# Fused self attention, cross attention and feed forward on one core: the first stage's q, k and v weights loaded and split by column quarters

## The reference

```python
h = _ln(x, g1, be1)
x = _attn(h, h, Wq1, Wk1, Wv1, Wo1, bo1) + x          # self attention
h = _ln(x, g2, be2)
x = _attn(h, context, Wq2, Wk2, Wv2, Wo2, bo2) + x    # cross attention
h = _ln(x, g3, be3)
y = h @ Wp + bp
a, gate = (y[..., :FF_HID], y[..., FF_HID:])
x = a * jax.nn.gelu(gate, approximate=False) @ W2 + b2 + x
# _attn: q = x@Wq, k = ctx@Wk, v = ctx@Wv; softmax(q k^T * DHEAD**-0.5) v; out @ Wo + bo
```

## Time and profile before

| | |
|---|---|
| median of 3 runs | 3026.1 us (3021.39 to 3029.89) |
| profiled execution | 3024.38 us, span 3022.6 us |
| PE busy | 2958.4 us (98% of the span) |
| DVE, ACT, POOL busy | 76%, 62%, 47% |
| first matmul on real data | 16.27 us after the span's start |

### The profile page before, as it was taken

The page is one execution under the profiler, slowest core; times in us unless marked ns, Lnnn a source line. Parts: engine busy times, 40 slices in busy tenths (PEclk is TensorE's granted clock), DMA queues, the critical chain, the costliest instruction groups (busy, mean ns, idle before and its releaser), DMA issues. The chain is left out here.

```text
span 3022.6 us, 77287 instructions
## 1 busy us (share of the span) xinstructions
PE 2958.4 (98%) x25480; PEld 2579.0 (85%) x25480; DVE 2304.4 (76%) x3858; ACT 1878.4 (62%) x5618; POOL 1429.0 (47%) x976
## 2 busy tenths in 40 slices
PE   7999999999999999999999999999999979999999
PEld 6888888888888888788888888888888858888888
DVE  5877777777777777788888888888888856666664
ACT  6666666666666666677777777777777733232322
POOL 4555555555555555555555555555555531111110
PEclk9999999999999999999999999999999989999999
DMA  7787878788887887888888888888888841112211
GB/s 239 228 243 243 243 244 244 243 243 246 244 245 240 245 247 239 261 252 256 253 253 254 253 254 253 254 251 260 251 252 254 248 148 56 56 62 62 69 56 35
DMA packets 475243, 640.79 MB, mean 212 GB/s; under 512 B 58944, under 2 KB 405952, under 8 KB 474944
## 3 DMA queue, kind: packets, MB, share of 16 engines
q1 hardware_dynamic: 473824, 639.96, 69.8%
q10 hardware_dynamic: 1376, 0.27, 0.1%
HBM read 338.57 MB, written 301.47 MB: 212 GB/s over the span
## 5 line engine op out<-in xcount | busy, mean ns | idle before, releaser
L602 POOL TENSOR_TENSOR at_probs<-at_probs,at_row_inv 128x1024 f32<-128x1024 f32 x512 | 969.6, 1894 | 1059.5 <-DVE at_row_inv L808 1059.4
L653 ACT ACTIVATE at_probs<-at_ps_s,at_neg_max 128x256 f32<-128x256 f32 x2048 | 945.7, 473 | 143.2 <-DVE at_neg_max L781 94.7
L781 DVE TENSOR_REDUCE at_neg_max<-at_ps_s 128x2 f32<-128x512 f32 x1024 | 660.4, 684 | 194.7 <-PE at_ps_s L959 191.1
L800 DVE STREAM_TRANSPOSE at_blocks<-at_probs 128x1024 f32<-128x1024 f32 x512 | 630.8, 1232 | 2.1 <-POOL at_probs L602 2.0
L706 ACT ACTIVATE at_qk_hi<-at_ps_qk 128x512 fp32r<-128x512 f32 x512 | 305.7, 597 | 324.5 <-PE at_ps_s L959 183.4
L978 PE MATMUL at_ps_o<-at_probs_t,at_v 128*64 128x256 f32 x4096 | 500.9, 386 | 1.9 <-DMA at_probs_t<-at_turns 1.9
L891 PE MATMUL at_ps_qk<-at_h_hi,w_hi 128*128 128x256 f32 x1536 | 432.1, 304 | 12.7 <-ACT at_h_hi L676 6.2
L653 ACT ACTIVATION_READ_ACCUMULATOR at_probs<-at_ps_s,at_neg_max 128x1 f32 x2048 | 414.6, 202 | 0.0
L978 PEld LDWEIGHTS at_ps_o<-at_probs_t,at_v 128*64 128x64 f32 x4096 | 271.9, 137 | 148.6 <-issue 3.2
L891 PE MATMUL at_ps_qk<-at_h_hi,w_lo 128*128 128x256 f32 x1536 | 397.9, 281 | 0.0
L891 PEld LDWEIGHTS at_ps_qk<-at_h_hi,w_hi 128*128 128x128 f32 x1536 | 290.1, 189 | 125.3 <-issue 104.5
(11 more groups left out here) (107 smaller groups left out, 6598.6 us busy)
## 6 DMA issues: line engine op xcount, KB each, us to landing
at_turns<-at_blocks SPq DMA_DIRECT2D x2048, 128.0 KB, 2.5
at_probs_t<-at_turns SPq DMA_DIRECT2D x512, 512.0 KB, 4.4
at_xt<-in_x SPq DMA_DIRECT2D x32, 256.0 KB, 5.4
at_xres<-in_x SPq DMA_DIRECT2D x32, 256.0 KB, 3.2
after_self_attention<-at_yout SPq DMA_DIRECT2D x32, 256.0 KB, 2.6
at_xt<-after_self_attention SPq DMA_DIRECT2D x32, 256.0 KB, 5.4
at_xres<-after_self_attention SPq DMA_DIRECT2D x32, 256.0 KB, 3.7
after_cross_attention<-at_yout SPq DMA_DIRECT2D x32, 256.0 KB, 2.6
```

The costliest lines, as they stand in the source:

```text
L602: pool.tensor_tensor(tile, tile, scale, ALU.mult).then_inc(probs_ready, 1)
L653: last = act.activation(probs[:, slot % 2, h, t], scores[:, slot % 2, h, t], ACT.Exp, bias=neg_max[:, slot % 2, i:i + 1], accum_out=row_su ...
L781: nc.vector.tensor_reduce(neg_max[:, slot, r], scores[:, slot, h], AX_X, ALU.max, negate=True).then_inc(neg_max_ready, 1)
L800: nc.vector.transpose(blocks[:, slot].rearrange("p (j a q) -> p a j q", j=QUADS, q=QUAD), probs[:, slot].rearrange("p h t (k j q) -> p (h ...
```

## The change

The loads of self attention's wq, wk and wv are cut into four column quarters each (256 columns of each of the two row blocks), and issued quarter by quarter; wo is still one load. ACT and DVE split quarter 0 before step 0 and quarters 1, 2 and 3 at the very end of steps 0, 2 and 4 of sequence 0, behind everything else these engines have in the step. PE waits at each step of sequence 0 for the quarter that it uses. wo's high part moves from before step 0 to the end of step 6 on ACT, its low part on POOL from before step 0 to step 6, ahead of `low_h(1)`. ACT waits for the self stage's two scale constants before `scale_shift(0)` and for the cross stage's two before step 0.

```diff
+    def quarter(self, source, w, i):
+        return source(w).rearrange("p (k n) -> p k n", k=KT)[:, :, i * V_COLS:(i + 1) * V_COLS]
+    def load_quarters(self, sp, quarter_loaded):
+        for i in range(4):
+            for w in WEIGHTS[:3]:
+                src = self.sources[w].rearrange("(k p) n -> p k n", p=P)
+                sp.dma_start(self.quarter(self.raw, w, i), src[:, :, i * V_COLS:(i + 1) * V_COLS]
+                             ).then_inc(quarter_loaded[w][i], 16)
+        sp.dma_start(self.raw("wo")...).then_inc(self.loaded["wo"], 16)
+    def split_high_quarter(self, act, w, i, quarter_loaded):
+        act.wait_ge(quarter_loaded[w][i], 16)
+        act.activation(self.quarter(self.hi, w, i), self.quarter(self.raw, w, i), ACT.Copy,
+                       scale=SCALE if w == "wq" else 1.0).then_inc(self.hi_ready[w], 1)
+    def split_low_quarter(self, eng, w, i):
+        eng.wait_ge(self.hi_ready[w], i + 1)
...
@@ sync
-            weights[SELF].load(sp)
+            weights[SELF].load_quarters(sp, quarter_loaded)
@@ gpsimd, step, ahead of low_h
+                if part == FIRST and p == 6:
+                    weights[SELF].split_low(pool, "wo")
@@ gpsimd, before sequences
-            weights[SELF].split_low(pool, "wo")
@@ scalar, end of step
+                if part == FIRST:
+                    for w in WEIGHTS[:3] if p < 6 else ():
+                        weights[SELF].split_high_quarter(act, w, p // 2 + 1, quarter_loaded)
+                    if p == 6:
+                        weights[SELF].split_high(act, "wo")
@@ scalar, before sequences
-            weights[SELF].split_high(act, "wq")
-            weights[SELF].split_high(act, "wk")
-            act.wait_ge(scales_loaded, 64)
+            weights[SELF].split_high_quarter(act, "wq", 0, quarter_loaded)
+            weights[SELF].split_high_quarter(act, "wk", 0, quarter_loaded)
+            act.wait_ge(scales_loaded[SELF], 32)
             scale_shift(0, SELF)
             high_h(0)
-            weights[SELF].split_high(act, "wv")
-            weights[SELF].split_high(act, "wo")
+            weights[SELF].split_high_quarter(act, "wv", 0, quarter_loaded)
+            act.wait_ge(scales_loaded[CROSS], 32)
@@ vector, end of step
+                if part == FIRST and p < 6:
+                    for w in WEIGHTS[:3]:
+                        weights[SELF].split_low_quarter(nc.vector, w, p // 2 + 1)
@@ tensor, project_v and, alike, wq and wk in project_qk
-                if part in (FIRST, SEAM) and p == 0:
-                    pe.wait_ge(weights[stage].lo_ready["wv"], 1)
+                if part == FIRST or part == SEAM and p == 0:
+                    pe.wait_ge(weights[stage].lo_ready["wv"], quarter + 1)
```

More of the change, by code:

```diff
@@ L163, in load @@
                              src.rearrange("(k p) n -> p k n", p=P)).then_inc(self.loaded[w], 16)
+    def quarter(self, source, w, i):
[6 more added lines that the diff above has]
+                             ).then_inc(quarter_loaded[w][i], 16)
+        sp.dma_start(self.raw("wo").rearrange("p (k n) -> p k n", n=DIM),
+                     self.sources["wo"].rearrange("(k p) n -> p k n", p=P)).then_inc(self.loaded["wo"], 16)
+    def split_high_quarter(self, act, w, i, quarter_loaded):
[4 more added lines that the diff above has]
+        eng.wait_ge(self.hi_ready[w], i + 1)
+        lo, raw, hi = (self.quarter(s, w, i) for s in (self.lo, self.raw, self.hi))
+        if w == "wq":
+            eng.scalar_tensor_tensor(lo, raw, SCALE, hi.bitcast(F32), ALU.mult, ALU.subtract
+                                     ).then_inc(self.lo_ready[w], 1)
+        else:
+            eng.tensor_tensor(lo, raw, hi.bitcast(F32), ALU.subtract).then_inc(self.lo_ready[w], 1)
     def split_high(self, act, w):
@@ L429, in attention @@
         scores = ps_s[:].rearrange("p (s h t k) -> p s h t k", s=2, h=2, t=TT)
-        scales_loaded = sem("scales_loaded")
+        scales_loaded = (sem("self_scales_loaded"), sem("cross_scales_loaded"))
+        quarter_loaded = {w: [sem(f"self_{w}_quarter_{i}_loaded") for i in range(4)] for w in WEIGHTS[:3]}
         biases_loaded = sem("biases_loaded")
@@ L639, in _ @@
                     act.dma_start(gamma_c[:, stage], gamma[stage].rearrange("(k p) -> p k", p=P)
-                                  ).then_inc(scales_loaded, 16)
+                                  ).then_inc(scales_loaded[stage], 16)
                     act.dma_start(beta_c[:, stage], beta[stage].rearrange("(k p) -> p k", p=P)
-                                  ).then_inc(scales_loaded, 16)
+                                  ).then_inc(scales_loaded[stage], 16)
             for stage in (SELF, CROSS):
@@ L860, in _ @@
             norm_stats(0)
-            for w in ("wq", "wk", "wv"):
-                weights[SELF].split_low(nc.vector, w)
+            for w in WEIGHTS[:3]:
+                weights[SELF].split_low_quarter(nc.vector, w, 0)
             sequences(nc, dve, n, step)
@@ L935, in project_qk @@
                     pe.wait_ge(qk_ready, c)
-                if part in (FIRST, SEAM) and p == 0:
-                    pe.wait_ge(weights[stage].lo_ready["wq"], 1)
+                if part == FIRST or part == SEAM and p == 0:
+                    pe.wait_ge(weights[stage].lo_ready["wq"], p // 2 + 1)
                 project_pair(ps_qk[:, 0:SEQ], p, stage, True, "wq", b + 1 if p == 0 else None)
-                if part in (FIRST, SEAM) and p == 0:
-                    pe.wait_ge(weights[stage].lo_ready["wk"], 1)
+                if part == FIRST or part == SEAM and p == 0:
+                    pe.wait_ge(weights[stage].lo_ready["wk"], p // 2 + 1)
                 first = stage == CROSS and p == 0
```

## The result

The changed kernel took 3042.96 us (median of 4, 3040.71 to 3044.93) against 3025.58 us before (median of 4): ratio 1.0057, interval 1.0043 to 1.0072, so 17 us slower. The profiled execution took 3040.71 us with a span of 3038.9 us, 16.3 us over that of before. PE's busy time hardly moved; against the earlier trace rows the page has 3 us more of it and the rest is idle time.

What follows compares the result with a forecast made beforehand. PE was taken as the bound, so ramp delays reach the end undiminished. Terms summed to +11.45 us without the clock, +13.65 with it, giving 3039.8 on the median of 3026.1; predicted 3039, range 3031 to 3046.

Steps and rivals of the forecast that it cites:

- 1 and 2, start and v: Prologue and step 0: PE starts earlier, -4.4 us, less +0.6 for POOL's xnorm; v no longer waits, -0.7.
- 3, wait at step 2: Sequence 0, step 2: PE waits for wq's quarter, split on DVE behind pair 0's maxima, +1.8 us.
- 4, wait at step 4: Sequence 0, step 4: quarter split behind ACT's exponentials, DVE also waiting for POOL's xnorm, +3.65 us.
- 5, wait at step 6: Sequence 0, step 6: quarter split after ACT is free, POOL idle, +2.7 us.
- 6, wait for `low_h`: Start of sequence 1: PE's h_lo pass waits for `low_h(1)`, which stands behind wo's splits, +7.8 us.
- 7, low clock behind the waits: PE at half rate behind the new long waits: two falls, +3.4 us, bounds 0 to 5.1.
- 7, earlier rise at the start: Early ramp: without the gap at v PE's clock can rise sooner, worth 0 to 2.5 us, taken as -1.2.
- POOL as the loser against DVE: Start: DVE's quarter splits lock out POOL's xnorm, moving it by 0 to 1.15 us, taken as +0.6.
- Rival B: Steps 4 and 6: ACT and DVE arrive earlier, each quarter as little as 1.8 us; +8.7, 3035 us; chance 0.12.
- Rival A: Sequence 1: the 3.59 us wait for o's low part swallows delay, giving 3.6 back; +7.9, 3034 us; chance 0.09.
- C: Sequence 1: no wo wait, because POOL reaches the split early; sum +3.7, or +2.5, 3029 us; chance 0.04.
- D: Whole ramp: faster, start gives 7.6 us, quarters and wo cost nothing; 3018 to 3019 us; chance 0.02.

Runs made afterwards that it cites:

- e9: Changed kernel with 16, 28, 22 and 60 unused filler matmuls in PE's four new waits, ending before each wait does; 3036.24 us, ratio 1.0039.
- e10: Changed kernel with ACT again waiting for all four scale constants before the first scale and shift; 3042.5 us, ratio 1.0062.
- e1: Kernel before, weights whole, with only the wait on scale constants split between self and cross stage; 3023.37 us, ratio 0.9999.
- e8: Changed kernel with quarters split early, wo's splits taken back from step 6, and DVE's first split waiting for POOL's xnorm; 3018.74 us, ratio 0.9986.
- e2: Kernel before with only wo's splits moved to step 6 of sequence 0, POOL's ahead of the next low part; 3033.01 us, ratio 1.0033.
- e3: Changed kernel with wo's splits taken back: ACT's to the end of step 0, POOL's ahead of the first normalisation; 3033.8 us, ratio 1.0032.
- e5: Changed kernel with POOL's order in step 6 turned: the next input's low part first, wo's low part behind it; 3039.64 us, ratio 1.0055.
- c0: Kernel before, unchanged, executed once more for a second profile; 3023.58 us in a single execution.

## Why the prediction was right

The forecast of 3039 us for 3042.96, in the range of 3031 to 3046, rests on a sum of +13.65; up to the mark 15.07 us were measured. In order of the prediction's terms:

| term | predicted | measured |
|---|---|---|
| 1 and 2, start and v (20.40 to 15.96) | -4.5 | -4.4 |
| 3, wait at step 2 (2.39 for 0.42) | +1.8 | +2.0 |
| 4, wait at step 4 (5.01 for 1.34) | +3.65 | +3.7 |
| 5, wait at step 6 (4.04 for 0.85) | +2.7 | +3.2 |
| 6, wait for `low_h` (7.36 for none) | +7.8 | +7.4 |
| 7, low clock behind the waits | +3.4 | +4.7 |
| 7, earlier rise at the start | -1.2 | -1.7 |

(The clock's shares are what the stretches between waits differ by: -1.66 from v to the wait of step 2, then +0.10, +1.04, +2.23 and +1.33; 0.28 us more in a small wait later complete the 15.07. In the stretches of +1.04 and +2.23 the kernel before has waits of 0.51 and 0.62 us that the changed kernel hasn't, so the low clock by itself costs more than the 4.7, nearer to the 5.5 us of e9.)

1. The start. Right in sum, but one premise failed: I held that the split of the constants' wait takes at_beta off the path. In the changed kernel all four constants are there before PE's transposes end, and the wait put back changes nothing (e10). The sum was right all the same, because it asked only that the constants be there before the transposes end, and that holds either way. The split wait alone, beside whole loads, moves PE's start by 1.2 to 2.6 us (e1). POOL as the loser against DVE, for which I had no row and took +0.6, is now seen: rstd takes 1.23 us instead of 0.72 and the second xnorm 1.37 instead of 1.04, together 0.8; e8 gives most of it back. By the rule of the Trainium skill (SBUF — State Buffer, "Who interferes with whom") whichever starts first locks the other out; the trace agrees, now in both directions, since DVE's quarter of wk takes 1.25 us there instead of 0.69 beside POOL's first xnorm.
2. Steps 2 to 6. Right, place by place, DVE's wait for POOL's xnorm in step 4 included. A quarter costs a bit more than a quarter of the whole: 0.63 us on ACT and 0.69 on DVE for 512 columns, where I put 0.5 and 0.57. From the end of ACT's exponentials to PE that makes 1.4 us for the 1.17 of the sum, 0.2 of the 0.5 missed at step 6; the rest stays open. Rival B, smaller delays, is out.
3. Sequence 1. Right in mechanism and size; e2 shows it alone, e3 takes it away and e5 exchanges it for one of 3.82 us.
4. The clock. The mechanism was right and its size too small, though inside its bounds: I counted two falls, and there was low clock behind the waits of step 4, step 6 and sequence 1. This is the larger part of the 1.4 us between my sum and the 15.07. Behind the 2.39 us wait of step 2, where I counted none, the changed kernel's profile has none either, but e3, e5 and e10, with the same wait, have it there, so that other executions of the changed kernel can pay a fourth. The spans differ by 1.2 us more than the mark does, 16.3 in all. Behind the mark the changed kernel's clock falls and that of the first profile of before does not, but c0's does, and such differences come without any change; that 1.2 us is not shown to be the change's.
5. Rival A, that the wait of 3.59 us in sequence 1 would shrink, is out: it is 3.59 again, since it moves along with PE's scores. C and D failed as argued.

The change's purpose was sound and its placing undid it: the same quarters in idle time, wo where POOL has nothing else to do, and POOL's norm ahead of DVE's first quarter give 0.9986.

## What to carry to other kernels

Splitting a prologue's work into pieces gains only if the pieces go where their engine idles; at the end of an in-order step they stand behind all that the step waits for, and the next step's first instruction pays. Before moving work ahead of another instruction on a side engine, follow who waits for that one: 6.4 us of splits that were free beside the first projections cost 7.4 us ahead of a 1.3 us subtraction. And count a wait on PE at more than its length, since the matmuls behind it may run at half the rate.

## What the runs showed of the hardware

- The landing of small constants goes with how the other queue's loads are cut. The two 1 KB loads of at_beta took 7.0 and 12.2 us beside loads with pieces of 4 KB and 4.0 and 5.8 us beside loads with pieces of 1 KB, the bytes asked for being the same. The longer of the two took 10.9 to 12.2 us in the four kernels with whole loads and 5.0 to 5.9 in the nine with cut ones. That the size of the pieces is the cause, and not their order, was not tried apart.
- A wait of 3.6 us on PE sometimes lowers its clock and sometimes doesn't, in the same place of the same program: at the mark of the kernel before, the first profile stays at 1.00 from 80 to 100 us, and c0 falls at 89.6. The fall can come behind the wait as well as in it: c0's first matmul takes 0.39 us at the mark and 0.58 at the change of stage, so the first matmul alone does not tell.
- A wait of 2.39 us was followed by low clock in three of the four profiles that have it without filler (a granted clock of 0.83 from 20 to 30 us in e3 and e10, 0.51 from 24 to 26 us in e5; 1.00 in the changed kernel's).
- Useless matmuls in the waits kept the fast level and saved some 5.5 us in the ramp.
